# Eight more down products in three parts, with GpSimd making their rests and SiLU kept in its PSUM bank

## What is computed

```
x = x + xattn(layernorm(x), ctx)        # scores normalised by mean and variance of a batch, softmax, @ Wo.T
y = layernorm(x)
probs = softmax(y @ gate_w + gate_b); cw = the two largest of 8, others 0
h  = y @ w1[e] + b1[e]                  # e = shared expert, then 8 routed ones; two halves a, b
out = sum over e of cw[e] * ((silu(a) * b) @ w2[e] + b2[e])     # cw = 1 for the shared expert
x = x + out
```

## Time and profile before

| | |
|---|---|
| median of 3 runs | 134.9 us (134.72 to 135.77) |
| the profiled execution | 135.15 us, its span 133.4 us |
| PE busy | 127.5 us (96%), granted clock 1.0 (the level of 2.4 GHz) throughout |
| DVE, ACT, POOL busy | 107.6, 84.8, 23.9 us |
| mean DMA | 97 GB/s |

### The profile page before, as it was taken

How to read it: one execution, slowest core, us unless ns; L and a number is a source line. 1 busy time by engine, 2 the same in 40 slices (tenths; PEclk the granted TensorE clock), 3 DMA queues, 4 the chain that set the end, 5 groups by cost and what they waited for, 6 DMA issues and landing times.

```text
span 133.4 us, 2135 instructions
## 1 busy us (share of the span) xinstructions
PE 127.5 (96%) x632; PEld 96.7 (72%) x632; DVE 107.6 (81%) x313; ACT 84.8 (64%) x165; POOL 23.9 (18%) x41
## 2 busy tenths in 40 slices
PE   7899999889999999999999999999999999999992
PEld 7677796858577776686788676598677667788871
DVE  1497788696997989999759997699697879989872
ACT  1557978996265389947653299956633987647250
POOL 7184154057700020602100020001200000000000
PEclk9999999999999999999999999999999999999999
DMA  3999400002910000098000002087000207910022
GB/s 107 304 331 269 149 7 0 0 2 86 337 59 0 0 0 2 10 296 328 0 5 0 0 0 79 18 292 332 2 0 0 79 5 182 403 44 5 0 79 79
DMA packets 8828, 12.97 MB, mean 97 GB/s; under 512 B 1321, under 2 KB 6994, under 8 KB 8306
## 3 DMA queue, kind: packets, MB, share of 16 engines
q1 hardware_dynamic: 8242, 12.62, 28.1%
q10 hardware_dynamic: 576, 0.23, 0.6%
HBM read 11.73 MB, written 1.11 MB: 96 GB/s over the span
## 4 chain that ended last, share of the span: by engine, by line
PE 61%; issue 15%; DVE 9%; ACT 7%; POOL 6%; DVEq 0%; POOLq 0%; ACTq 0%
PE bank L998 55%; ACT prob L508 3%; POOL w_rest L434 3%; POOL ln_rstd L419 2%; PE bank L1062 1%; PE bank L1014 1%; ACT L553 1%; PE bank L1113 1%; PE bank L1090 1%; DVE x L902 1%; ACT act_head L580 1%; PE bank L1181 1%; DVE g_beats L824 1%; DVE g_rank L827 1%; ACT silu L588 1%
## 5 line engine op out<-in xcount | busy, mean ns | idle before, releaser
L588 ACT ACTIVATE silu<-bank,b_cols 128x512 f32<-128x512 f32 (+1 forms) x37 | 24.8, 676 | 23.7 <-PE bank L998 23.2
L998 PE MATMUL bank<-x_head,w_head 128*128 128x512 f32 x72 | 33.7, 468 | 0.3 <-issue 0.3
L998 PE MATMUL bank<-x_head,w_rest 128*128 128x512 f32 x72 | 28.5, 395 | 0.0
L998 PE MATMUL bank<-x_rest,w_head 128*128 128x512 f32 x72 | 28.5, 395 | 0.0
L881 DVE SCALAR_TENSOR_TENSOR act<-bank,b_cols,silu 128x512 f32<-128x512 f32 (+1 forms) x34 | 24.9, 734 | 1.3 <-DVE silu L873 0.3
L873 DVE TENSOR_TENSOR silu<-silu,cw_all 128x512 f32<-128x512 f32 (+1 forms) x28 | 18.6, 668 | 3.3 <-ACT silu L588 2.6
L998 PE MATMUL bank<-act,w_sb 128*128 128x512 f32 x38 | 19.4, 592 | 0.0
L998 PEld LDWEIGHTS bank<-x_head,w_head 128*128 128x128 f32 x72 | 13.6, 189 | 5.3 <-issue 2.7
L998 PEld LDWEIGHTS bank<-x_rest,w_head 128*128 128x128 f32 x72 | 13.6, 189 | 3.9 <-issue 1.9
L998 PEld LDWEIGHTS bank<-x_head,w_rest 128*128 128x128 f32 x72 | 13.5, 188 | 3.3
L890 DVE TENSOR_TENSOR act_rest<-act,act_head 128x512 fp32r<-128x512 f32 x15 | 10.0, 685 | 4.1 <-ACT silu L588 2.0
(11 more groups left out here) (130 smaller groups left out, 219.4 us busy)
## 6 DMA issues: line engine op xcount, KB each, us to landing
cw_all<-cw_dram SPq DMA_DIRECT2D x4, 1024.0 KB, 7.0
cw_all<-cw_dram SPq DMA_DIRECT2D x4, 512.0 KB, 5.0
cw_all<-cw_dram SPq DMA_DIRECT2D x6, 256.0 KB, 3.7
x_sb<-in_x_dram SPq DMA_DIRECT2D x4, 256.0 KB, 4.2
w_sb<-in_L_ffn_rw_dram SPq DMA_DIRECT2D x1, 1024.0 KB, 7.4
ctx_sb<-in_ctx_dram SPq DMA_DIRECT2D x4, 192.0 KB, 4.2
out_dram<-x SPq DMA_DIRECT2D x3, 256.0 KB, 2.1
w_sb<-in_L_ffn_rw_dram SPq DMA_DIRECT2D x1, 512.0 KB, 7.1
```

Source lines behind the costliest of these rows:

```text
L588: scalar.activation(silu[:, k, cols], hid(n, 0)[:, cols], ACT.Silu, bias=b1_cols[:, 0, e:e + 1]).then_inc(silu_sb, 1)
L998: return pe.matmul(dst, lhs, rhs, start=start, stop=stop, skip_group_check=True)
```

## The change

1. **More products in parts.** DIVIDED takes slots 4, 6, 12, 13, 15, 21, 22 and 24 in addition (23 instead of 15 slots). ACT gets 8 more casts, all placed "first", ahead of silu(m+2); PE replaces 8 float32 products by three passes each.
2. **GpSimd makes their rests**, in two halves of 256 columns each, in slot m+1 of its own list. `clear_of_vector` holds it until a named small step of DVE is over. DVE keeps the 15 rests that it had.
3. **The rest of w2** goes from DVE to GpSimd (slot 3, two instructions), its heads on ACT from slots 5 and 6 to slot 2.
4. **SiLU in its bank.** For most slots from 4 on (not e = 0, not e = 1 from the second chunk on, not slot 35), SiLU overwrites half a in PSUM, and DVE's product with the weights reads it there and writes SBUF. Half a of slot n+2 then waits for scaled(n), not for silu(n). For e = 1, raw(n) overwrites half b in the same way.
5. `scores_rstd` of GpSimd moves one slot later, behind the rests of its slot.

```diff
-        POOL_AT = {'first_rstd': [-9, 1], 'scores_rstd': [-2, 0], 'second_rstd': [4, 0]}
+        POOL_AT = {'first_rstd': [-9, 1], 'scores_rstd': [-1, 1], 'second_rstd': [4, 0]}
...
         DOWN_BEHIND, CLOSE_FROM = 3, NX * (C - 1) + 1
-        DIVIDED = [n for n in range(NX - 1, LAST - STRAIGHT)
-                   if n >= NX * (C - 1) or n % NX in ((0, 1, 2, 7, 8) if n < NX * 2 else (0, 7, 8))]
+        DIVIDED_OF = [(4, 6, 8), (0, 1, 2, 3, 4, 6, 7, 8), (0, 3, 4, 6, 7, 8), range(NX - STRAIGHT - 1)]
+        DIVIDED = [n for n in range(NX * C) if n % NX in DIVIDED_OF[n // NX]]
+        BY_POOL = [n for n in DIVIDED if n < NX * (C - 1) and n % NX in (3, 4, 6)]
+        BY_DVE = [n for n in DIVIDED if n not in BY_POOL]
...
-            return {7: "first", 2: "last"}.get(m % NX, "between")
-
-        def divided_in(n, places):
-
-            return [m for m in range(n - 2, n) if m in DIVIDED and parts_slot(m) == n and parts_place(m) in places]
+            return {3: "first", 4: "first", 6: "first", 7: "first", 2: "last"}.get(m % NX, "between")
+
+        def heads_in(n, places):
+
+            return [m for m in DIVIDED if parts_slot(m) == n and parts_place(m) in places]
+
+        def dve_rests_in(n, places):
+            return [m for m in BY_DVE if parts_slot(m) == n and parts_place(m) in places]
+
+        def weighted(n):
+
+            c, e = n // NX, n % NX
+            return E * c + e - c
+
+        def in_bank(n):
+
+            return FOUR_BANKS_FROM <= n < LAST and n % NX >= (1 if n < NX else 2)
...
+            def w2_rests():
+                for g, (lo, hi) in enumerate(W2_GROUPS):
+                    pool.wait_ge(w2_head_sb, g + 1)
+                    pool.tensor_tensor(w2_rest[:, lo:hi, :], w2_sb[:, lo:hi, :], w2_head[:, lo:hi, :].bitcast(F32), ALU.subtract).then_inc(w2_rest_sb, 1)
+
+            def clear_of_vector(m):
+
+                c, e = m // NX, m % NX
+                if e == 3:
+                    pool.wait_ge(shift_sb, c + 2)
+                elif e == 4 and c + 2 < C:
+                    pool.wait_ge(simstat_sb, c + 3)
+                elif e == 4:
+                    pool.wait_ge(gz_sb, C)
+                elif e == 6:
+                    pool.wait_ge(cw_sb, c + 2)
+
+            def act_rests(m):
+                pool.wait_ge(act_head_sb, divided(m))
+                for cols in (slice(0, N // 2), slice(N // 2, N)):
+                    pool.tensor_tensor(act_rest[:, m % 3, cols], act[:, m % 4, cols], act_head[:, m % 3, cols].bitcast(F32), ALU.subtract).then_inc(pool_rest_sb, 1)
...
+                if n == 3:
+                    pool.wait_ge(shift_sb, 2)
+                    pool.wait_ge(scaled_sb, weighted(n))
+                    w2_rests()
+                if n - 1 in BY_POOL:
+                    clear_of_vector(n - 1)
+                    act_rests(n - 1)
                 for piece, c in due(POOL_AT, n, 1):
...
-                    scalar.activation(silu[:, k, cols], hid(n, 0)[:, cols], ACT.Silu, bias=b1_cols[:, 0, e:e + 1]).then_inc(silu_sb, 1)
+                    silu_out = hid(n, 0)[:, cols] if in_bank(n) else silu[:, k, cols]
+                    scalar.activation(silu_out, hid(n, 0)[:, cols], ACT.Silu, bias=b1_cols[:, 0, e:e + 1]).then_inc(silu_sb, 1)
...
-                if n in (5, 6):
-                    w2_heads(n - 5)
+                if n == 2:
+                    w2_heads(0)
+                    w2_heads(1)
...
+                dve.scalar_tensor_tensor(hid(n, 1)[:, :], hid(n, 1)[:, :], b1_cols[:, 1, 1:2], silu[:, k, :], ALU.add, ALU.mult).then_inc(raw_act_sb, 1)
+                between()
                 dve.wait_ge(y_ps, n - 3)
-                dve.scalar_tensor_tensor(act[:, n % 4, :], hid(n, 1)[:, :], b1_cols[:, 1, 1:2], silu[:, k, :], ALU.add, ALU.mult).then_inc(raw_act_sb, 1)
-                between()
                 dve.wait_ge(cw_in[cw_group(1)], 16 * arrivals(c, cw_group(1)))
                 dve.wait_ge(raw_act_sb, c)
-                dve.tensor_tensor(act[:, n % 4, :], act[:, n % 4, :], cw_all[:, 0, :], ALU.mult).then_inc(act_sb, 1)
+                dve.tensor_tensor(act[:, n % 4, :], hid(n, 1)[:, :], cw_all[:, 0, :], ALU.mult).then_inc(act_sb, 1)
...
-                        dve.tensor_tensor(silu[:, k, cols], silu[:, k, cols], cw_all[:, e - 1, cols], ALU.mult).then_inc(scaled_sb, 1)
+                        dve.tensor_tensor(silu[:, k, cols], hid(n, 0)[:, cols] if in_bank(n) else silu[:, k, cols], cw_all[:, e - 1, cols], ALU.mult).then_inc(scaled_sb, 1)
...
-                if n == NX:
-                    w2_rests()
                 run(n, 2)
...
-                    pe.wait_ge(silu_sb, n - 1)
+                    if in_bank(n - 2):
+                        pe.wait_ge(scaled_sb, weighted(n - 2))
+                    else:
+                        pe.wait_ge(silu_sb, n - 1)
...
                 if n in DIVIDED:
-                    pe.wait_ge(w2_rest_sb, 1)
-                    pe.wait_ge(act_rest_sb, divided(n))
+                    pe.wait_ge(w2_rest_sb, len(W2_GROUPS))
+                    if n in BY_POOL:
+                        pe.wait_ge(pool_rest_sb, 2 * (BY_POOL.index(n) + 1))
+                    else:
+                        pe.wait_ge(act_rest_sb, BY_DVE.index(n) + 1)
```

More of the change, by code:

```diff
@@ L171, in xattn_moe_kernel @@
         act_sb, raw_act_sb, y_ps = sem("act_sb"), sem("raw_act_sb"), sem("y_ps")
-        act_head_sb, act_rest_sb = sem("act_head_sb"), sem("act_rest_sb")
+        act_head_sb, act_rest_sb, pool_rest_sb = sem("act_head_sb"), sem("act_rest_sb"), sem("pool_rest_sb")
         out_ps, outt_sb, tok_ps, final_sb = sem("out_ps"), sem("outt_sb"), sem("tok_ps"), sem("final_sb")
@@ L662, in _ @@
                     pieces[piece](k)
-                for m in divided_in(n, ("first",)):
+                for m in heads_in(n, ("first",)):
                     act_heads(m)
@@ L666, in _ @@
                     expert_silu(c, e)
-                for m in divided_in(n, ("between",)):
+                for m in heads_in(n, ("between",)):
                     act_heads(m)
@@ L674, in _ @@
                     pieces[piece](k)
-                for m in divided_in(n, ("last",)):
+                for m in heads_in(n, ("last",)):
                     act_heads(m)
-                if n in (5, 6):
-                    w2_heads(n - 5)
+                if n == 2:
+                    w2_heads(0)
+                    w2_heads(1)
             out_bias(C - 1)
@@ L876, in expert_gate @@
                     if e >= 1:
-                        dve.wait_ge(scaled_sb, E * c + e + h - c)
+                        dve.wait_ge(scaled_sb, weighted(n) + h)
                     dve.wait_ge(b_ps, n + 1)
@@ L882, in expert_gate @@
                                              ALU.add, ALU.mult).then_inc(act_sb, 1)
-            def w2_rests():
-                dve.wait_ge(w2_head_sb, len(W2_GROUPS))
-                dve.tensor_tensor(w2_rest[:, :, :], w2_sb[:, :, :], w2_head[:, :, :].bitcast(F32), ALU.subtract).then_inc(w2_rest_sb, 1)
             def act_rests(n):
@@ L977, in between @@
                 def between():
-                    for m in divided_in(n, ("first", "between")):
+                    for m in dve_rests_in(n, ("first", "between")):
                         act_rests(m)
@@ L985, in _ @@
                     expert_gate(c, e, between)
-                for m in divided_in(n, ("last",)):
+                for m in dve_rests_in(n, ("last",)):
                     act_rests(m)
```

## The result

The changed kernel takes 136.04 us (median of 7 runs, 135.93 to 136.18). The kernel before, run beside it, takes 135.40 (7 runs, 134.72 to 135.77). The ratio is 1.0055, 95% interval 1.0034 to 1.0076, so the change costs about 0.74 us (0.46 to 1.03). The profiled execution took 136.04 us, its span 134.3, where before it was 135.15 and 133.4.

A forecast was written before the change was run, and what follows sets the result against it. PE's work plus its waits was taken to bound the kernel. Delays of +0.90, savings of -0.39 and +0.15 sum to +0.66 on 134.9, so 135.5 us; own range 135.1 to 135.9, whole range 134.0 to 136.4.

The forecast's parts named there:

- The savings of down(4), down(6), down(13) and down(15) are lost: Ahead of slot 10's half b and down(16): what these products save on PE is lost in its waits there.
- The five other casts: ACT, slots 4, 12, 13, 21 and 22: casts fall into ACT's holes and cost nothing; without that cover, 0.62 each.
- The waits for scaled(n): PE, half a of slot n+2: the new wait costs nothing by itself, at most 0.05 us.
- the run of ACT hides 0.65 of it: Slot 14: ACT's run hides 0.65 us of a DVE stall, so only a longer stall reaches PE.
- the rival in which GpSimd's rests stop DVE: Slot 14: GpSimd's rests of act(12) hold DVE for 1.4 us, 0.75 reaches PE; 136.3 us, chance 0.13.
- a hole of DVE ahead of sim_sq: Slot 14: sign that the forecast is wrong, DVE idle ahead of sim_sq while GpSimd subtracts.
- The bank: SiLU written into PSUM: taken as nothing, bounds from 0.3 us off the sum to 0.3 added.
- cast of act(6): First turn, ahead of silu(8): the cast makes PE's half b of slot 10 later by 0.45 us.
- down(12) in parts: PE, ahead of silu(16): gives back 0.16 us, so silu(16) comes 0.29 late in place of 0.45.
- cast of act(15): Second turn: ACT's run gets 0.61 us longer, so silu(18) and down(16) come 0.90 late.
- down(21), down(22), down(24): PE, after slot 22: products in parts save 0.16, 0.07 and 0.16, together 0.39 us.
- cast of act(24): Third chunk: cw_rows' wait of 0.46 for PE takes most of the cast's 0.61 us; some 0.15 remain.

The follow-up runs named there:

- e3: Changed kernel with slots 6, 15 and 24 float32 again and GpSimd holding act(12)'s rest until DVE's small operations of slot 14 are over: 134.83 us, ratio 0.9966.
- e6: Changed kernel with the divided slots of the kernel before, leaving SiLU in its bank, w2's rest on GpSimd and small moves: 135.29 us, ratio 0.9996.
- e4: Kernel before plus three casts on ACT, of act(6), act(15) and act(24), ahead of the table loads into an unread tile: 136.54 us, ratio 1.0098.
- e7: Changed kernel with act(15) cast twice, the first time into a tile that nothing reads: 136.54 us, ratio 1.0092.
- e9: Changed kernel with act(12)'s rest held until DVE's small operations of slot 14 are over, and slot 15 undivided: 135.18 us, ratio 0.9991.
- e12: e3 with slot 12 undivided, so that nothing has to be held back: 134.83 us, ratio 0.9959.
- e2: Changed kernel with GpSimd holding act(12)'s rest back until DVE's small operations of slot 14 are over: 135.83 us, ratio 1.0035.
- e1: Changed kernel with slots 6, 15 and 24 back to float32 products, so no cast at the turns: 135.32 us, ratio 1.0000.
- e5: Changed kernel with SiLU written to SBUF everywhere, as before, all else the same: 136.68 us, ratio 1.0102.
- e8: Changed kernel with each of GpSimd's rests in four pieces of 128 columns in place of two of 256: 136.15 us, ratio 1.0066.
- e11: e3 with slot 13 undivided, so no rest of act(13) is made by GpSimd: 134.73 us, ratio 0.9954.

## Why the prediction was right, and where it was not

**The number.** 135.5 was forecast as +0.66 on 134.9. It came out at +0.55%, 0.74 us, within 1% and inside the range. The 136.04 is measured on another base (135.40 in these runs), so the difference is what counts: 0.74 lies in the forecast's own +0.2 to +1.0, while 136.04 itself lies just above its 135.1 to 135.9. The bound was read rightly: less work for PE, 1.0 against 1.10 forecast, and its idle time higher by 1.9 (forecast 1.7), lost at the two turns. But the closeness is in part luck: several terms were off, in both directions, and one that is as large as half of the result was put at nothing (the sum below).

**Right.** A down product in parts saves 0.16. The savings of down(4), down(6), down(13) and down(15) are lost: e3 saves two of these and down(12) and has the same distances up to down(16) as e6. The casts at the two turns reach PE through silu(8) and through silu(18), rest(16) and down(16) (e4, e7, e9). The five other casts cost nothing that a distance shows (e3 against e6). GpSimd is in time everywhere, down(6) too: its rest ends at 53.61 and the product starts at 53.75. The waits for scaled(n) cost nothing that a distance shows (e6 against before).

**Two sizes.** The sum took 0.61 a cast. A cast puts off down(16) by 0.49 to 0.52. At the first turn it puts off half b of slot 10 by 0.26, where the prediction had 0.45, and silu(16) by 0.36 to 0.39. The profile before could have said so. This is a row of ACT there:

```profile
56.67 1.16 ACT L580 CAST act_head<-act 128x512 fp32r<-128x512 f32 x2
```

Two casts together take 1.16, so that one more adds 0.54 and not the 0.62 of a single row. The mistake was to use starts on PE and durations on ACT. The other size is down(12): it was to give back 0.16 ahead of silu(16) and gives nothing (e12 against e3, 42.06 and 42.05), for the reason that follows.

**The step that failed: "the run of ACT hides 0.65 of it".** It stood in the rival in which GpSimd's rests stop DVE. The sign that the prediction gave for it, a hole of DVE ahead of sim_sq, did not show as a hole but as a longer row. The stall came, 0.40 long, below the 0.65 from which it was to count, and it cost 0.4 us: e2 takes it away and gains 0.43 up to silu(16), e1 keeps it and is 0.38 behind before. The prediction looked at DVE's work in ACT's run and overlooked a wait of PE's ahead of that run: the product for the score averages stands before half a of slot 16 and waits for the logits. In the trace before, these are DVE's logits and PE's product:

```profile
75.45 0.19 DVE L810 TENSOR_TENSOR logits<-bank,logits_part 128x32 f32<-128x32 f32 x1
```
```profile
75.79 0.37 PE L998 MATMUL bank<-sim_mom,mean_of_partitions 128*128 128x16 f32 x2
```

From start to start 0.34, and no wait is shown, so it looked free. After, where PE does wait for the logits, the distance is 76.63 - 76.29 = 0.34 as well: it had been a tie. So DVE's logits set half a of slot 16 in both kernels. What makes them late makes ACT's whole run late, and what PE saves ahead of them, down(12) too, comes to nothing.

The Trainium skill (SBUF — State Buffer, "Who interferes with whom"), cited in that rival as a lock under which the later of the two waits until the other is over, is borne out in both directions here: DVE's sim_sq ends when GpSimd's half is over (0.57 against 0.17), in e5 GpSimd's rest takes 1.87 against 1.42, and with SiLU read from a bank neither waits. That DVE gets in between two pieces with a single operation is what e8 adds, at the one place where it was seen.

**The bank.** It was put at nothing, with 0.3 each way. By itself it is nothing that the times can tell (e6), though SiLU takes 0.66 into a bank against 0.69 and ln_rstd 1.01 against 1.39. Together with the rests on GpSimd it is worth 0.47%, 0.63 us (e5 against the changed kernel): not a gain but the cover for the other part, which the prediction did not price. It noted that the change frees GpSimd for the scaled products; it did not ask what the change would cost without that. The 0.22 that it gives back behind down(16) was put at nothing as well.

**The sum again, by distances:**

| term | forecast | measured |
|---|---|---|
| cast of act(6) | +0.45 | +0.37 |
| down(12) in parts | -0.16 | 0 |
| the stall in slot 14 | 0 | +0.40 |
| cast of act(15) | +0.61 | +0.49 |
| SiLU in its bank | 0 | -0.22 |
| down(21), down(22), down(24) | -0.39 | -0.48 |
| cast of act(24) | +0.15 | +0.26 |
| sum | +0.66 | +0.82 |

The first and the third are a division of the 0.77 up to silu(16), for which e1, e2 and e4 give 0.38 to 0.43 each. The two of the last stretch are 3 x 0.16 and what is left of its 0.22; down(22) saves as much as the others, counted with its transposes, and not 0.07. The forecast's total was nearer than its parts.

## What to carry to other kernels

Take the cost of one more instruction from the distance between starts on its engine, and follow every wait that shows no idle time just ahead of the run that bounds: a tie is a wait with no slack. Look at what VectorE runs beside work that is given to GpSimd: here it was 0.63 us cheaper with VectorE's product reading PSUM. Holding such work back until the short VectorE operations are over paid here; cutting it in smaller pieces did not. And PE time saved ahead of a place where another engine sets the pace is not saved: e11 divides 19 down products, the changed kernel 23, and e11 takes 1.4 us less by the distances.

## What was unexpected of the hardware

- A cast that follows a short read on ACT starts 0.09 us behind that read's start, a table load 0.22 behind it. A cast added between them puts the load off by 0.51, a second one by 0.51 (82.00 to 82.51 in e7).
- ACT writes SiLU of 512 columns into PSUM in 0.66 us, into SBUF in 0.69.
- VectorE's wait for GpSimd shows in the profile as a longer operation (0.57 us for 8 elements) and not as idle time; the profile's list of waits doesn't name it.
